# Storing x to the output ahead of the second FFN and scattering its weighted results onto it with an add

## What is computed

```python
x = x + 0.5 * ffn(layernorm(x))
x = x + attn(layernorm(x))
x = x + 0.5 * ffn(layernorm(x))
# ffn: probs = softmax(x @ w_router); sel = argmax(probs); wgt = probs[sel]
for e in range(8):
    y = relu(xt @ w1[e] + b1[e]) @ w2[e] + b2[e]
    out = out + ((sel == e) * wgt)[:, None] * y
```

## Time and profile before

| | us |
|---|---|
| median of 3 runs (526.37 to 531.33) | 527.44 |
| the profiled execution, its own time | 530.52 |
| its span in the trace | 528.7 |
| TensorE busy | 402.7 |
| VectorE busy | 324.6 |
| ScalarE busy | 215.6 |
| GpSimd busy | 189.3 |

### The profile page before, as it was taken

How to read it: one execution, slowest core, us unless ns; L and a number is a source line. 1 busy time by engine, 2 the same in 40 slices (tenths; PEclk the granted TensorE clock), 3 DMA queues, 4 the chain that set the end, 5 groups by cost and what they waited for, 6 DMA issues and landing times.

```text
span 528.7 us, 9840 instructions
## 1 busy us (share of the span) xinstructions
PE 402.7 (76%) x2994; PEld 335.7 (63%) x2995; DVE 324.6 (61%) x963; ACT 215.6 (41%) x555; POOL 189.3 (36%) x171
## 2 busy tenths in 40 slices
PE   4438699906998799896999896988999860069990
PEld 4312599904776678675778675767777850069990
DVE  3571477667159788279785388783788425037763
ACT  2531244415454373453444544544455501024430
POOL 4265044520005532214543034243054433715450
PEclk9999699957999898999879998999999555569995
DMA  8999122130000000000000000000004000112215
GB/s 282 218 407 178 35 72 70 50 90 2 0 1 1 2 1 0 2 0 0 0 0 0 0 0 0 0 0 0 1 2 159 1 1 20 50 46 67 70 50 169
DMA packets 26108, 27.06 MB, mean 51 GB/s; under 512 B 2946, under 2 KB 23042, under 8 KB 25698
## 3 DMA queue, kind: packets, MB, share of 16 engines
q1 hardware_dynamic: 22002, 17.98, 13.2%
q0 software_dynamic: 2496, 5.13, 3.3%
q10 hardware_dynamic: 1584, 3.63, 1.9%
HBM read 17.52 MB, written 9.21 MB: 51 GB/s over the span
## 4 chain that ended last, share of the span: by engine, by line
PE 48%; DVE 17%; DMA 10%; POOL 9%; issue 8%; ACT 6%; DVEq 0%; ACTq 0%; SPq 0%; POOLq 0%
PE bank L777 45%; POOL slots L471 6%; DMA slots<-QKT 4%; ACT WVT L672 2%; DMA slots<-XN,POS 2%; DMA QKT<-by_token 1%; PE bank L856 1%; DVE CS L1552 1%; DMA WR<-w_router 1%; DVE X L1178 1%; POOL HS L497 1%; DVE W1R L1574 1%; DVE HS L1576 1%; PE bank L967 1%; DVE HS L1583 1%
## 5 line engine op out<-in xcount | busy, mean ns | idle before, releaser
L497 POOL TENSOR_TENSOR HS<-HS,MHALF 128x8 f32<-128x8 f32 x16 | 26.3, 1644 | 199.8 <-DVE HS L1584 199.8
L477 POOL DMA_INDIRECT by_token<-YB,IDX x46 | 43.9, 955 | 67.8 <-DVE YB L1291 67.2
L777 PE MATMUL bank<-XBT,W1R 128*128 128x128 f32 x368 | 52.8, 290 | 0.1
L672 ACT ACTIVATE WVT<-bank,AC 128x128 f32<-128x128 f32 x128 | 36.5, 374 | 36.1 <-PE bank L777 36.1
L777 PE MATMUL bank<-W,HT 128*128 x368 | 49.9, 280 | 0.0
L777 PEld LDWEIGHTS bank<-XBT,W1R 128*128 128x128 f32 x368 | 48.0, 204 | 0.9 <-ACT XBT L580 0.6
L777 PEld LDWEIGHTS bank<-W,HT 128*128 128x128 f32 x368 | 46.1, 197 | 0.3
L471 POOL DMA_INDIRECT slots<-XN,POS x32 | 31.3, 978 | 28.5 <-DMA slots<-QKT 11.4
L856 PE MATMUL bank<-K,XB 128*128 128x128 f32 x46 | 13.5, 297 | 35.0 <-DMA XB<-slots 35.0
L580 ACT ACTIVATE XBT<-bank 128x128 f32<-128x128 f32 x46 | 12.8, 277 | 65.4 <-PE bank L856 42.8
L636 ACT ACTIVATE QKT<-bank,COLS 128x512 f32<-128x512 f32 x32 | 22.0, 688 | 40.8 <-PE bank L777 40.8
(11 more groups left out here) (289 smaller groups left out, 1027.9 us busy)
## 6 DMA issues: line engine op xcount, KB each, us to landing
W<-w SPq DMA_DIRECT2D x2, 2048.0 KB, 7.7
slots<-QKT SPq DMA_DIRECT2D x2, 1483.5 KB, 20.6
XB<-slots SPq DMA_DIRECT2D x46, 64.5 KB
W<-w SPq DMA_DIRECT2D x1, 2064.0 KB
QKT<-by_token SPq DMA_DIRECT2D x8, 256.0 KB, 3.7
X<-x SPq DMA_DIRECT2D x4, 256.0 KB, 5.8
out<-X SPq DMA_DIRECT2D x4, 256.0 KB, 2.3
by_token<-YB,IDX POOLq DMA_INDIRECT x46
```

The lines of the kernel that those rows point to most:

```text
L477: g.indirect_dma_start(out=by_token[f], out_offset=bass.IndirectOffsetOnAxis(ap=IDX[:, j:j + 1], axis=0), in_=YB[:, j, :], in_offset=None) ...
L497: step.do(g.tensor_tensor(HS[:, 3, :], HS[:, 2, :], MHALF[:, 0:H], ALU.pow))
L672: ins = a.activation(DT[:, hf, m, :], DM[:, m * P:(m + 1) * P], ACT.Exp, bias=AC[:, c, h:h + 1])
L777: return t_.matmul(o, l, r, start=start, stop=stop, skip_group_check=True)
```

## The change

Only the second FFN changes. x is stored to the output before its blocks run (SyncE, behind the load of W2). A token's weight travels with the token, in a further column 129 of XN, `slots` and XB. VectorE copies it for each block into WT and multiplies the block's result by it. GpSimd scatters the results onto the output itself, with an add on the way, and leaves out rows whose number is over 2047. `by_token` is no longer read for f = 1, nor are its rows added to X, and the four stores at the end are gone. GpSimd waits for the weights before it scatters tokens, and for the stores of x before it scatters results. So that the weights are ready by then, the exponentials are taken sooner, in 16 instructions on ScalarE that read the logits in PSUM, scale, shift and sum at once, and VectorE's `shift` moves ahead of the maximum.

```diff
-SLOT = D + 1
+SLOT = [D + 1, D + 2]
...
                     sp.wait_ge(pj_full, NB * NPJ)
                     sp.dma_start(W2[:, :, :, :], w2).then_inc(w2_loaded, 16)
+                    for q in range(4):
+                        sp.wait_ge(*tr_read_at(NB - 1 if q == 3 else NB - 2, "d3"))
+                        sp.dma_start(out_v[:, 4 * q:4 * q + 4, :], X[:, 4 * q:4 * q + 4, :]).then_inc(out_stored, 16)
...
-                for q in range(4):
-                    sp.dma_start(YG[:, 4 * q:4 * q + 4, :], by_token[f][512 * q:512 * (q + 1), :]
-                                 .rearrange("(t p) d -> p t d", p=P)).then_inc(y_loaded[f][q], 16)
-            for g in range(4):
-                sp.wait_ge(ffn_done[1], 4 * g + 4)
-                sp.dma_start(out_v[:, 4 * g:4 * g + 4, :], X[:, 4 * g:4 * g + 4, :]).then_inc(out_stored, 16)
+                    for q in range(4):
+                        sp.dma_start(YG[:, 4 * q:4 * q + 4, :], by_token[512 * q:512 * (q + 1), :]
+                                     .rearrange("(t p) d -> p t d", p=P)).then_inc(y_loaded[q], 16)
             sp.wait_ge(out_stored, 64)
...
                 pool.wait_ge(pos_ready[f], 1)
+                if f == 1:
+                    pool.wait_ge(weights_ready, 1)
...
+                if f == 1:
+                    pool.wait_ge(out_stored, 64)
                 for k in range(NBLK):
...
+                        g.indirect_dma_start(out=out, out_offset=at, in_=YB[:, j, :], in_offset=None,
+                                             bounds_check=NT * P - 1, oob_is_err=False, compute_op=ALU.add)\
+                            .then_inc(y_sent[f][j], 16)
...
+                    for t in range(NT):
+                        a.activation(EX[:, t, :], bank[3][:, t * NE:(t + 1) * NE], ACT.Exp, scale=LNA[:, 5, t:t + 1],
+                                     bias=LNA[:, 7, t:t + 1], accum_out=RT[:, 2, t:t + 1]).then_inc(exp_ready[f], 1)
...
+                if f == 1:
+                    shift(f, 1)
                 do(v.tensor_reduce(RT[:, 0, :], logits, AX_X, ALU.max))
                 do(v.tensor_tensor(OH[:, :, :], logits, bc(RT[:, 0, :], [P, NT, NE]), ALU.is_equal))
+                if f == 1:
+                    v.scalar_tensor_tensor(out=LNA[:, 7, :], in0=RT[:, 0, :], scalar=-1.0, in1=LNA[:, 5, :],
+                                           op0=ALU.mult, op1=ALU.mult).then_inc(shifted[f], 1)
...
+                    dve.wait_ge(exp_ready[f], NT)
+                    do(v.reciprocal(RT[:, 3, :], RT[:, 2, :]))
+                    v.tensor_scalar(XN1[:, :, D + 1], RT[:, 3, :], 0.5, None, ALU.mult).then_inc(weights_ready, 1)
...
+                    if f == 1:
+                        v.tensor_copy(WT[:, j:j + 1], XB[:, j, D + 1:D + 2])
                     v.tensor_copy(IDX[:, j:j + 1], XB[:, j, D:D + 1]).then_inc(idx_copied[f], 1)
...
+                        v.tensor_tensor(YB[:, j, :], bank[6 + j % 2][:, 0:D], B2R[:, j, :], ALU.add)\
+                            .then_inc(y_summed, 1)
+                        dve.wait_ge(y_summed, k + 1)
+                        dve.wait_ge(idx_copied[f], k + 1)
+                        v.tensor_scalar(YB[:, j, :], YB[:, j, :], WT[:, j:j + 1], None, ALU.mult)\
+                            .then_inc(y_ready[f], 1)
```

More of the change, by code:

```diff
@@ L96, in macaron @@
     out_v = out.rearrange("(t p) d -> p t d", p=P)
-    slots = [nc.dram_tensor(f"slots_{f}", [NBLK * P, SLOT], F32, kind="Internal").ap() for f in range(2)]
-    by_token = [nc.dram_tensor(f"by_token_{f}", [NT * P + NBLK * P, D], F32, kind="Internal").ap() for f in range(2)]
+    slots = [nc.dram_tensor(f"slots_{f}", [NBLK * P, SLOT[f]], F32, kind="Internal").ap() for f in range(2)]
+    by_token = nc.dram_tensor("by_token", [NT * P + NBLK * P, D], F32, kind="Internal").ap()
     with ExitStack() as ctx:
@@ L127, in macaron @@
             second.enter_context(nc.sbuf_tensor("BEFORE_XN1", [P, NE * FC * D + 4 * HID], F32))
-            XN1 = second.enter_context(nc.sbuf_tensor("XN1", [P, NT, SLOT], F32))
+            XN1 = second.enter_context(nc.sbuf_tensor("XN1", [P, NT, SLOT[1]], F32))
         WQH, WKH, WSKH = (sb(name, [P, 2, HID], F32R) for name in ("WQH", "WKH", "WSKH"))
@@ L287, in macaron @@
         y_full, y_ready, y_sent = per_ffn("y_full"), per_ffn("y_ready"), per_ffn_ring("y_sent")
-        y_loaded, ffn_done = per_ffn_ring("y_loaded"), per_ffn("ffn_done")
+        y_summed = sem("y_summed")
+        y_loaded, ffn_done = [sem(f"y_loaded_{q}") for q in range(4)], sem("ffn_done")
         folds_ready, fold_full, folds_split = sem("folds_ready"), sem("fold_full"), sem("folds_split")
@@ L374, in _ @@
             sp.wait_ge(fill_made, 1)
-            sp.dma_start(slots[0].rearrange("(k p) w -> p k w", p=P), FILL).then_inc(slots_filled[0], 16)
+            sp.dma_start(slots[0].rearrange("(k p) w -> p k w", p=P), FILL[:, :, 0:SLOT[0]]).then_inc(slots_filled[0], 16)
             sp.dma_start(COLS[:, :], colpack).then_inc(cols_loaded, 16)
@@ L389, in _ @@
                     sp.dma_start(W2[:, :, :, :], w2).then_inc(w2_loaded, 16)
+                    for q in range(4):
+                        sp.wait_ge(*tr_read_at(NB - 1 if q == 3 else NB - 2, "d3"))
+                        sp.dma_start(out_v[:, 4 * q:4 * q + 4, :], X[:, 4 * q:4 * q + 4, :]).then_inc(out_stored, 16)
                 def load_block(k, j):
[L392 removed]
+                    sp.dma_start(XB[:, j, 0:SLOT[f]], slots[f][bass.ds(k * P, P), :]).then_inc(xb_loaded[f][j], 16)
                 def turn(k, j, n):
@@ L1172, in moments, with combine @@
                                           op0=ALU.mult, op1=ALU.add))
-            def combine(f, q):
-                dve.wait_ge(y_loaded[f][q], 16)
+            def combine(q):
+                dve.wait_ge(y_loaded[q], 16)
                 for t in range(4 * q, 4 * q + 4):
                     v.scalar_tensor_tensor(out=X[:, t, :], in0=YG[:, t, :], scalar=RT[:, 3, t:t + 1],
-                                           in1=X[:, t, :], op0=ALU.mult, op1=ALU.add).then_inc(ffn_done[f], 1)
-                dve.wait_ge(ffn_done[f], 4 * q + 4)
+                                           in1=X[:, t, :], op0=ALU.mult, op1=ALU.add).then_inc(ffn_done, 1)
+                dve.wait_ge(ffn_done, 4 * q + 4)
             def layer_moments(f, group):
@@ L1223, in ffn @@
                     .then_inc(onehot_ready[f], 1)
-                shift(f, 1)
+                if f == 0:
+                    shift(f, 1)
                 dve.wait_ge(ranks_full[f], 1)
@@ L1311, in ffn @@
                     low_weights()
-                combine(f, 0)
-                if f == 0:
+                    combine(0)
                     norm_moments(0)
                     scale_norm(0)
-                    combine(0, 1)
+                    combine(1)
                     low_xt(0)
-                for q in range(2 - f, 4):
-                    combine(f, q)
+                    for q in range(2, 4):
+                        combine(q)
             def gate_masks():
```

45 lines of the change are left out of this document (27 added, 18 removed).

## The result

| | before | after | ratio, 95% interval |
|---|---|---|---|
| median, us (20 runs each, one chip) | 527.03 (525.43 to 531.33) | 529.60 (527.35 to 532.15) | 1.0041 [1.0022, 1.0060] |
| profiled execution, own time | 530.52 | 530.06 | |
| its span | 528.7 | 528.2 | |
| from the second FFN's logits to the end | 92.76 | 95.37 | |

The changed kernel is 2.6 us slower. The forecast was 521.4, with a range up to 529.0, so the measured time lies outside it and on the other side of before. The two profiled spans hide the loss, because what lies ahead of the second FFN differs from execution to execution: the logits came at 435.87 before and at 432.80 after. "Result ready" is the end of the last operation on YB, the product where there is one.

A forecast was written before the change was run, and what follows sets the result against it. TensorE sets the block loop at 1.913 us a turn, VectorE having 0.21 us of slack, before an uncovered tail. Terms -10.6 + 0.5 + 3.15 + 0.95 = -6.0 us take the 527.4 median to 521.4, range 518 to 529.

The forecast's parts named there:

- Removed, -10.6: End of the second FFN: table loads, adds to X and final stores go, saving 10.6 us, all on the path.
- The adding scatter, +0.95: Last result scatter: with the add it lands 3.2 us after its start instead of 2.25, costing 0.95 us.
- the last result's wait, +0.15: End of the blocks: the last result's product, net of its scatter's shorter wait behind its neighbour, costs 0.15 us.
- the ring: Block loop's four result buffers: a scatter's landing stays hidden from VectorE up to 4.4 us.
- Added in a block, +3.7 and -0.7: Block loop: VectorE's turn of 2.10 us exceeds TensorE's 1.913, 3.7 us over 20 turns; the last turns return 0.7.
- Added before the scatters, +0.5: Routing: VectorE's extra steps and the wait for the weights start the first token scatter 0.5 us later.
- "dear" rival: Routing: exponentials at 0.41 us each start the token scatters 2.0 us later, giving 523.4 us; chance 0.13.
- Moved for nothing: Stores of x moved behind the W2 load: covered by over 25 us, so they cost nothing.
- The clock: TensorE in the block loop: granted clock 1.00, which might not stay there once TensorE has gaps.
- The loop did not keep its time: Rival for the block loop: it keeps its time, with a turn of 1.97 us or less, giving 518.4; chance 0.12.
- The slow scatter: Rival: result scatters landing beyond 4.4 us make VectorE wait every turn; 529.6 us at a 5 us landing; chance 0.20.
- Its other half: Rival's GpSimd side: each result scatter doubles to 2.56 us and bounds the loop, giving 531.9; within the 0.20 chance.

The follow-up runs named there:

- e1_before_no_tail: Kernel before with only the tail taken away: x stored early, plain scatters to the table, nothing read back; 519.05 us against 523.26, ratio 0.9923.
- e8_pool_waits: Changed kernel with GpSimd waiting until its last scatters have landed before its closing DRAIN; 528.46 us against 525.32 for the kernel before, ratio 1.0072.
- e2_no_product: Changed kernel without VectorE's product by the weight and the weight's copy in each block; 522.48 us against 523.26 for the kernel before, ratio 0.9970.
- e5_early_weights: Changed kernel with VectorE subtracting, scaling and summing, and one ScalarE exponential in place of 16; 526.08 us against 525.32 for the kernel before, ratio 1.0023.
- e12_all: Changed kernel with one exponential, ScalarE's product, b2 add before the copies, VectorE's block loop written out; 521.08 us against 524.00 before, ratio 0.9944.

## Why the prediction was wrong, step by step

- **Removed, -10.6.** This step failed, and it is over half of the miss (4.9 of 8.6 us). It said that behind the last landing "nothing is left but its semaphore". The end of the program is the later of two chains, and I priced only the one that the chain of waits showed. GpSimd's closing DRAIN ended at 523.11 in before, 5.4 us ahead of the end, under cover of the table's loads and stores. With the cover gone it is the end: 8.19 from the last scatter's start, where I had 3.2 (and 0.1). The tail gave 4.7 and not 9.65. e1_before_no_tail shows the loss with no adding scatter, product or new routing in it, e8_pool_waits that the DRAIN is not the landing.
- **The adding scatter, +0.95, and the last result's wait, +0.15.** The landing was forecast well: the last one took 2.8 against 3.2, and the ring held but for 0.4 us. What was mis-sized is the other end, the second largest part of the miss (2.1). The last product was to cost 0.15 net of the queue ahead of its scatter; it cost 0.33 by itself, and the queue grew by 1.9. That the add and the limit might cost GpSimd more stood among the rivals with a doubling to 2.56 a scatter; a smaller rise had no term in the sum. The instruction takes 1.56 in place of 0.96, and starts 0.78 behind its result in place of 0.28. In the middle of the loop both fit under a turn, but the last results come less than 1.86 apart and queue. In none of these traces do results pile up behind GpSimd before the last three, so it isn't the bound of the loop.
- **Added in a block, +3.7 and -0.7.** The mechanism was right: VectorE becomes the bound, e2_no_product takes 3.8 out of the blocks again, and each new piece has the size forecast (0.06 for 0.08, 0.32 for 0.32, 0.28 for 0.28). From the first transpose to the relu of block 21 the loop grew by 4.5 against 3.7. The turn I read off has no branch in it: turns without one came out at 2.01 to 2.19 against the forecast's 2.10, but one in four is about 2.7, and the mean of the last eighteen is 2.23. In before, too, one turn of four was 2.1 to 2.4, and TensorE's queue of work hid it; when VectorE itself sets the pace, nothing does. The last turns gave back 0.5 and not 0.7 (3.27 from that relu to the last add, where I had 3.06 and before 3.78). That the whole miss here is only 1.0 is partly luck: the first two turns were 0.95 shorter than before, which I had not forecast. By the rule of the Trainium skill ("VectorE: DVE Perf Modes", What auto-detection actually checks) the product would have been like the copy, 0.23; the trace has 0.28 to 0.29, and the measurement decides.
- **Added before the scatters, +0.5.** It was 1.2. The exponentials took 0.345 each and not 0.2, since the sum is a second instruction; they ended 0.6 behind POS. This lies between the forecast and the "dear" rival, and e5_early_weights wins 0.87 back.
- **Moved for nothing.** Right: from the first scatter of tokens to the first transpose 23.49 against 23.61, and nothing waits for the stores.
- **The clock** stayed at 1.00 in the loop, as forecast though left open.
- **Rivals.** The loop did not keep its time. The slow scatter, given 0.20, has just the measured time (529.6), but that is chance: its landing was to be 4.8 or more, and the last one took 2.8, while the medians of all adding scatters are 3.2 to 3.4 in the five traces that list them. Its other half, a dearer scatter on GpSimd, did come, but smaller, and told only at the last three. The rival that decided it, another engine's end hidden beside the tail, wasn't on the list.

## What to carry to other kernels

Before a tail is priced as gone, look in the view of closing instructions for what each engine does until its own end: the saving is only the distance to the next-latest one, and here GpSimd needs 6.45 us behind its last scatter, so its last work should come early. When an engine has a few tenths of slack in a turn, take its turn as a mean over the loop, branch included, and not from one clean instance. Before an instruction is moved within a turn or to another engine, follow who waits for what stands behind it all the way round: a ring of waits over two engines set a turn of 2.08 us with neither engine full.

## What the runs showed of the hardware

- GpSimd's closing DRAIN took 6.44 us once all its scatters had landed, and ended 6.45 us behind the last scatter's record in every other trace, with plain and adding scatters alike.
- An indirect scatter of 128 rows that adds cost GpSimd 1.56 us against 0.96; the limit on indices changed nothing in that (1566 and 1563 ns). The last one landed 2.8 us after its start against 2.25 before; the median from issue to landing was 3.2 to 3.4 for adding ones and 2.2 for plain ones of the same runs, and one of e12_all took 5.06.
- A scatter with the limit on indices, onto the output, started 0.78 us after its result was ready, with the add or without; without a limit, onto the table by token, 0.28, adding or plain.
- On ScalarE the output of a sum is a second instruction: a pair on 128x8 came every 0.345 us, sixteen in 5.5 us, where one exponential of 128x128 took 0.31.
- On VectorE the branch of a loop and a register load between instructions left VectorE idle for up to 0.6 us; behind the product the load left 0.63, behind the index copy 0.29 to 0.42. They are seen only once VectorE sets the pace.
